# PSUM banks from one table of users, two heads per 32 columns, merged gate, rank and FFN projections, and new instruction lists in a one-core decoder block

## What is computed

```python
# 1 attention, 16 heads of 16, linear, with decay per head and a carried state
q, k = rotate(silu(x @ Wq)), rotate(silu(x @ Wk)); v = x @ Wv
scores = einsum('bthd,bshd->bhts', qi, ki) * D          # D: causal decay
o = scores @ v + (qi * decay_q) @ S;  S = lam_C * S + (ki * decay_k).T @ vi
o = group_rmsnorm(o * sigmoid(x @ Wg1 @ Wg2)) * weight
x = layernorm(x + o @ Wo)
# 2 experts: the token's number chooses one of 4; weights are ctx[e]
y = (silu(x @ Wg[e].T) * (x @ Wu[e].T)) @ Wd[e].T
x = layernorm(x + y)
# 3 FFN: positions are the FOUR sequences (l = 4), the 256 tokens are its batch
u = silu(prev(x) * conv_w[:, 0] + x * conv_w[:, 1])
q = rotate(silu(u @ Wq)); k = rotate(u @ Wk)            # 16 heads of 8
v = u @ Wv; g = u @ Wg
# each position picks one of two routes; causal sum over pairs (l, m), m <= l
o = sum_m (q_l . k_m) * same_route(l, m) * weight_l * v_m
x = layernorm(x + (silu(g) * head_norm(o)) @ Wout)
```

## Time and profile before

| | us |
|---|---|
| median of 3 runs | 193.52 |
| lowest and highest | 191.72, 193.52 |
| the profiled execution | 193.44 |
| its span, first to last instruction | 191.0 |
| around the span (193.44 - 191.0) | 2.44 |
| PE busy | 167.1 (87%) |
| DVE busy | 116.7 (61%) |
| POOL busy | 95.0 (50%) |
| ACT busy | 83.8 (44%) |

### The profile page before, as it was taken

How to read it: one execution, slowest core, us unless ns; L and a number is a source line. 1 busy time by engine, 2 the same in 40 slices (tenths; PEclk the granted TensorE clock), 3 DMA queues, 4 the chain that set the end, 5 groups by cost and what they waited for, 6 DMA issues and landing times.

```text
span 191.0 us, 3630 instructions
## 1 busy us (share of the span) xinstructions
PE 167.1 (87%) x1182; PEld 119.0 (62%) x1182; DVE 116.7 (61%) x318; ACT 83.8 (44%) x217; POOL 95.0 (50%) x175
## 2 busy tenths in 40 slices
PE   7699999999899999968968993989776999899870
PEld 7367476567577868747857892665352575588650
DVE  3156648995799779675312114260968959999731
ACT  2128362435155553344433522665546365542452
POOL 8957942431330566756640032624388524634682
PEclk9999799999999999999999999699999799999997
DMA  5999466000000001150537833211120000000113
GB/s 150 337 392 386 166 191 193 7 0 2 3 2 3 0 31 55 33 165 0 189 117 217 289 109 102 75 37 55 36 74 29 0 0 3 0 0 2 53 54 113
DMA packets 12417, 17.52 MB, mean 92 GB/s; under 512 B 1840, under 2 KB 8560, under 8 KB 12272
## 3 DMA queue, kind: packets, MB, share of 16 engines
q1 hardware_dynamic: 9056, 12.75, 20.5%
q10 hardware_dynamic: 2576, 2.46, 3.8%
q0 software_dynamic: 768, 2.10, 3.6%
HBM read 11.54 MB, written 5.77 MB: 91 GB/s over the span
## 4 chain that ended last, share of the span: by engine, by line
PE 54%; DVE 13%; POOL 10%; DMA 10%; issue 8%; ACT 4%; POOLq 0%; SPq 0%; DVEq 0%; ACTq 0%
PE bank L1462 20%; PE bank L1547 8%; PE bank L1457 4%; PE bank L1575 3%; PE bank L1692 3%; DMA xT<-in_x_turned 3%; DMA ys_d<-qkr 2%; PE bank L1767 2%; PE bank L1785 2%; PE bank L1569 2%; DMA yg<-ys_d,pos 2%; POOL yg L478 2%; POOL rstd L425 2%; PE bank L1677 2%; PE bank L1595 2%
## 5 line engine op out<-in xcount | busy, mean ns | idle before, releaser
L1462 PE MATMUL bank<-f_w,oT 128*128 128x512 f32 (+4 forms) x80 | 30.5, 534 | 2.4 <-ACT oT L773 2.4
L408 POOL TENSOR_TENSOR rsin<-qk,rope_tab 128x256 f32<-128x256 f32 x16 | 13.8, 879 | 23.5 <-ACT qk L643 23.5
L1462 PEld LDWEIGHTS bank<-f_w,oT 128*128 128x128 f32 x80 | 15.6, 207 | 14.6 <-issue 8.3
L1063 DVE TENSOR_TENSOR probs<-bank,con 128x512 f32<-128x512 f32 x32 | 20.6, 683 | 6.4 <-PE bank L1547 6.3
L1547 PE MATMUL bank<-qx,kT 32*128 32x256 f32 x128 | 18.4, 404 | 0.7 <-DVE probs L1063 0.7
L1462 PE MATMUL bank<-w_qk,xT 128*128 128x512 f32 x32 | 16.9, 655 | 1.6 <-DMA xT<-in_x_turned 1.6
L478 POOL DMA_INDIRECT yg<-ys_d,pos x8 | 8.1, 1007 | 18.7 <-DMA ys_d<-qkr 17.3
L1547 PEld LDWEIGHTS bank<-qx,kT 32*128 32x128 f32 x128 | 11.4, 188 | 6.7 <-issue 5.9
L1677 PE MATMUL bank<-xsT,slot_w 128*128 128x128 f32 x112 | 14.6, 284 | 0.2 <-issue 0.2
L1166 DVE TENSOR_TENSOR rsin<-rcos,bank 128x512 f32<-128x512 f32 (+1 forms) x8 | 4.9, 616 | 15.5 <-ACT rcos L744 15.5
L1677 PEld LDWEIGHTS bank<-xsT,slot_w 128*128 128x128 f32 x112 | 13.8, 197 | 0.7 <-issue 0.4
(11 more groups left out here) (155 smaller groups left out, 361.3 us busy)
## 6 DMA issues: line engine op xcount, KB each, us to landing
slot_w<-in_ctx_turned SPq DMA_DIRECT2D x14, 256.0 KB, 3.0
xs_d<-xs SPq DMA_DIRECT2D x2, 896.0 KB, 12.5
xs<-xs_d SPq DMA_DIRECT2D x6, 256.0 KB, 3.0
ys_d<-qkr ACTq DMA_DIRECT2D x6, 256.0 KB, 3.1
xT<-in_x_turned SPq DMA_DIRECT2D x4, 256.0 KB, 6.6
x_sb<-in_x SPq DMA_DIRECT2D x1, 1024.0 KB, 9.1
out<-x_sb SPq DMA_DIRECT2D x8, 128.0 KB, 1.7
w_qk<-in_w_qk ACTq DMA_DIRECT2D x1, 512.0 KB, 3.9
```

Source lines behind the costliest of these rows:

```text
L408: eng.tensor_tensor(dst[:, :, s, :], src[:, :, 1 - s, :], tab[:, :, s, :], ALU.mult)\
L1063: eng.tensor_tensor(probs[:, i % 2, :, :].rearrange("p (f r h) n -> p f r h n", f=KT, h=2)[:, :, g, :, :], bank[3 + g % 2][:, :].rearrange ...
L1462: last = eng.matmul(dst, lhsT[:, k, :], w[:, k, :], start=(k == 0), stop=(k == KT - 1))
```

## The change

- A table `BANKS` lists, for each of the eight banks, all its users in order; `at(kind, i)` gives the bank and `free(eng, kind, i)` waits for the reading of the user before it in the table. All fixed banks and their waits are gone, and buffers that were laid over others (`zsil`, `aT`, `ys`, `prev`, `conv`, `uT`) have their own memory.
- `scores(i)` is one step for all four 32-row groups into four banks. `attend(i)` is one step: two heads share 32 output rows (the values of each padded with zeros on the other's side and summed in PSUM). `oT` has 256 columns instead of 512, `turn_back` two transposes instead of four, `state` 128 columns instead of 256 per half, and its clearing is gone. `turn_q` and `turn_k` are one `turn_qk` in one bank.
- `gate_low` and `proj_gate` are once for all eight tiles, with four column or row groups. The gate is Tanh of half its input, and `gate_o` multiplies by (tanh + 1); the factor 2 goes into the root's epsilon.
- `rank_tokens` is two matmuls; DVE makes the running sums (`earlier_in`) first, in four more small steps. `inverse_root` has nine steps instead of eleven.
- The FFN projects each key once and rotates the query (`turn_query`, POOL, three instructions, for l < 3). `project_values` and `project_route` replace `project_step`: 384 or 512 and 400 or 272 columns.
- `keep_input` puts the residual's matmul first in each output group, as one matmul of up to 512 columns.
- All five lists are written anew; SP issues `fetch_second(0)` and `fetch_second(1)` ahead of the loads of chunk 1.

```diff
+BANKS = [
+    "qk.1 gate.2 qk.4 back.1 qk.6 on.0 sc.21 qkT.6 sc.26 sc.29 back.6 z.0 wo.6 y.1 xsT.5 z.5 xsT.7 f1.1 h2T.5 sum.0 fT.0",
...
+        def free(eng, kind, i):
+            if before_it[kind, i] is not None:
+                for name, value in last_read(*before_it[kind, i]):
+                    eng.wait_ge(S_(name), value)
...
-                eng.memset(state[:, :, :, :], 0.0).then_inc(S_("state_zeros"), 1)
...
+            def turn_query(j):
+                c, l = j // L, j % L
+                n = c * (L - 1) + l
+                eng.wait_ge(S_("fq_copied"), j + 1)
+                if n:
+                    eng.wait_ge(S_("q_turned"), 2 * n)
+                eng.tensor_tensor(q_parts[:, :, :].rearrange("p s (h d) -> p s h d", d=HK), ..., ALU.mult)
+                eng.wait_ge(S_("q_parts"), n + 1)
+                for half in range(2):
+                    eng.tensor_tensor(heads(fqr[:, c, l, :], HK)[:, :, a], ..., ALU.subtract)
...
+            def tanh_gate(n):
+                eng.wait_ge(S_("gate_made"), n + 1)
+                eng.activation(gate[:, 2 * n:2 * n + 2, :], two(at("gate", n)[:, :]), ACT.Tanh, scale=0.5)
...
+            def gate_low():
+                for k in range(KT):
+                    for n in range(4):
+                        last = eng.matmul(at("low", 0)[32 * n:32 * n + 32, 0:D], w_g1[:, k, :], xT[:, 2 * n:2 * n + 2, k, :],
...
+            def scores(i):
+                for g in range(4):
+                    free(eng, "sc", 4 * i + g)
                 for f in range(KT):
-                    for half in range(2):
-                        rows_ = slice(64 * r + 32 * half, 64 * r + 32 * half + 32)
+                    for g in range(4):
+                        rows_ = slice(32 * g, 32 * g + 32)
+                        last = eng.matmul(at("sc", 4 * i + g)[:, f * D:(f + 1) * D], kT[rows_, i % 2, f, :],
...
+            def attend(i):
+                free(eng, "o", i)
+                eng.wait_ge(S_("probs"), 4 * i + 4)
                 for f in range(KT):
+                    if i >= L:
+                        for n in range(4):
+                            eng.matmul(out_[n], state[:, i - L, f, 32 * n:32 * n + 32], qp[:, i % 2, f, :],
+                    for s in range(2):
+                        for n in range(4):
+                            last = eng.matmul(out_[n], v_sb[:, i % 3, 4 * f + n, s:s + 2, :].rearrange("p a e -> p (a e)"),
+                                              probs[:, i % 2, 8 * f + 2 * n + s, :], ...)
...
+                eng.matmul(at("rank", 0)[:, 0:n + m], ones[:, :], earlier_in[:, :, :].rearrange("p b e -> p (b e)"),
+                           start=True, stop=False)
+                eng.matmul(at("rank", 0)[:, 0:n], causal, onehot..., start=False, stop=True)
...
+            def project_route(j):
+                a, n = (0 if l == 0 else P), D + H + P * (l < 2)
+                project(at("f2", j)[:, 0:n], uT[:, j % 2, :, :], f_w2[:, :, a:a + n])
+            def project_values(j):
+                a, n = (0 if l == 2 else P), 3 * P + P * (l >= 2)
+                project(at("f1", j)[:, 0:n], uT[:, j % 2, :, :], f_w1[:, :, a:a + n])
...
+            def keep_input(g):
+                eng.wait_ge(S_("h2_done"), L * c + l1)
+                free(eng, "fout", g)
+                eng.matmul(at("fout", g)[:, 0:(l1 - l0) * D], ident, h2[...], start=True, stop=False)
```

More of the change, by code:

```diff
@@ L1861, in _ @@
[L1861 to L1874 removed]
+            project_o(1)
+            scores(5)
+            attend(4)
+            transpose_on(2)
+            transpose_on(3)
+            turn_qk(6)
@@ L1875, in _ @@
+            project_o(2)
+            project_o(3)
+            attend(5)
+            scores(6)
+            turn_back(4)
+            turn_qk(7)
+            proj_v(6)
+            turn_back(5)
+            scores(7)
+            proj_v(7)
+            attend(6)
+            attend(7)
             turn_back(6)
-            attend(7, 0)
+            turn_back(7)
+            turn_slots(0)
             transpose_on(4)
-            attend(7, 1)
+            transpose_on(5)
             project_o(4)
-            turn_back(7)
```

1083 lines of the change are left out of this document (473 added, 610 removed), and 7 rows, old and new, of the table BANKS.

## The result

The changed kernel takes 174.55 us (median of 4 runs, 172.41 to 175.71), the kernel before, measured with it, 193.52. The ratio of the two is 0.8958, 95% interval 0.8832 to 0.9084. The profiled execution took 175.22 us, its span is 173.4. Executions of this kernel differ in where TensorE's granted clock falls (0.965 on average in this one), so what follows compares stages, and names the clock of each.

What follows compares the result with a forecast made beforehand. In attention TensorE was taken to set the pace, with VectorE close behind. Stages of 71.0, 20.6, 32.7, 42.0 and 4.8 gave a 171.1 us span, with 2.44 around it 173.5 us; range 166 to 183.

Steps and rivals of the forecast that it cites:

- Stage 1: From the start to the end of the last attend: 80.83 us before, predicted 71.0, a gain of 9.8.
- the first mask at about 15.3: In attention, VectorE's first mask was to start at about 15.3 us, against 25.37 before.
- Rival 1: In attention, scores stay at two row groups at a time, so TensorE keeps 8.5 us more: 183 us; chance 0.08.
- Stage 2: From the last attend's end to chunk 1's slots on TensorE: 22.1 us before, predicted 20.6, a gain of 1.5.
- Stage 3: From chunk 1's slots on TensorE to the FFN's first pair product: 31.4 us before, predicted 32.7, 1.3 longer.
- The narrower projections at nothing: In the FFN, 2.6 us less projection work per chunk was taken as hidden; if TensorE were the bound, worth 5.2.
- Stage 4: From the first pair product to the last statistics: 51.9 us before, predicted 42.0, a gain of 9.9.
- Stage 5: From the last statistics to the span's end (last root, finish, store): 4.8 us, predicted to stay.
- Rival 2: In attention, waits for a bank's previous reader hold TensorE at 0.80 busy: 181.5 us; chance 0.15.
- Rival 3: In the FFN, POOL becomes the bound; 2.5 us of waits stay and 3.5 are added: 179.5 us; chance 0.17.
- Rival 4: Both engines pack better, with Stage 1 at 67 us and Stage 4 at 39: 166.5 us; chance 0.15.
- Rival 5: Gaps in more places often drop TensorE to 1.2 GHz, slower than before: 198.5 us at 25 us; chance 0.03.

Runs made afterwards that it cites:

- e9: Changed kernel with every score product issued twice into the same place: 181.91 us, ratio 0.9319 to the kernel before.
- e4: Changed kernel with the second item's weights for chunk 1 fetched behind the loads of chunk 1's slots: 176.21 us, ratio 0.9192 to the kernel before.
- b3: Changed kernel with token numbers loaded second, 8 filler products ahead of transpose_h2(0), and fetch_second(1) behind chunk 1's slot loads: 168.57 us, ratio 0.8716 to the kernel before.
- e2: Changed kernel with mark_experts moved later in VectorE's list, between rope_cos(1) and rope_add(1): 172.95 us.
- b2: e2 plus 8 and 5 unread filler products on TensorE ahead of transpose_h2(0) and slots_down(7): 173.95 us, ratio 0.9035 to the kernel before.
- e7: Changed kernel with the FFN's route projection issued twice for positions 0 and 1 of each chunk: 178.66 us.
- e5: Changed kernel without keep_input, the residual added last in its group of sums as before the change: 178.78 us.
- e6: Changed kernel with the rotation of the FFN query (turn_query) and its waits left out: 172.82 us, ratio 0.8851 to the kernel before.
- e8: Changed kernel with the gates as Sigmoid instead of Tanh of half the argument, constants adapted: 174.39 us, ratio 0.9075 to the kernel before.
- e1: Changed kernel with the 16 score products of each tile in another order: 173.86 us, ratio 0.904 to the kernel before.
- e3: Changed kernel with chunk 1's last expert item moved ahead of the first FFN step: 176.38 us, ratio 0.9158 to the kernel before.
- e10: Changed kernel with the 4 KB of token numbers loaded second instead of fifth: 172.2 us, ratio 0.8763 to the kernel before.

## Why the prediction was right, and where its steps were off

**Stage 1: the mark right, one input wrong.** Scores took 1.15 us a tile where I had 1.06; the work fell from 18.4 to 9.1 us, so 9.3 went where I had 8.5. The Trainium skill, TensorE: Matmul & The Clock Gate, section Measured speedup vs the span model, gave 1.12: its rule of 3.07 instead of 4 is nearer than mine, and the trace agrees with it. That VectorE would take over at 0.85 was too low a share; it reached 0.95. What failed is "the first mask at about 15.3". I followed rotation, transpose and scores, and did not follow mark_experts, which the new list moves ahead of all VectorE work, up to the DMA it waits for. With the fall of the clock behind it, the first mask came 4.5 us late. The two errors cancelled, and that the mark was met to 0.8 us is luck: 48 us of VectorE work from 15.3 at a share of 0.95, and attend(7) behind it, would have ended near 67, and with the tokens early it did (66.35). Rival 1 is refuted by the 1.15 us and, for its price, by e9.

**Stage 2: the gain was not there.** I had the last scatter at +15.1 us after the last attend; it was issued at +16.0 (86.20). And I took 2.5 us for its landing, as before, where it took 3.78. With the second item's weights fetched behind the slots it took 2.40 (e4) and 2.39 (b3). That this fetch, which now starts beside the scatter, is what slows it is shown by those two against 3.71 to 3.92 us in the eleven others; the step that failed is that I carried over a DMA time without asking what runs beside it. The other 0.9 us lies on POOL. It began the last two scale_o at +4.4, near my +4.6, but the last scatter came 11.6 us behind that. My own pieces (1.2, 5.0 and three scatters of 1.3) give 10.1, and the +15.1 I wrote allows 10.5; 0.83 us of the 11.6 is a wait for VectorE's statistics. No run varied it.

**Stage 3: right but for the clock.** Gather(4) at +22.3 and the 10.5 us from there (four gathers 5.2, two ln_scale 2.5, two rotations 2.8). Where TensorE kept its clock, gather(4) came at +22.28 (e2), +22.75 (b2) and +22.47 (b3), and the stage took 33.0, 33.5 and 33.2 against 32.7. From gather(4) on it was 10.75. In the changed kernel's own profile gather(4) came at +24.6, behind a granted clock of 0.51 from 110 to 116 us; that is 2.3 of the 2.7 us missed. An earlier step was wrong without harm: gather(0) was to come at +8.6 and came at +10.3, at +9.6 to +10.0 in the three with a kept clock, so the 1.1 us gained on the kernel before's +9.7 weren't there. I had priced the clock only as the rival that loses everything, and left it out of the forecast's own terms. "The narrower projections at nothing" was right for stage 4 and wrong for stage 3: e7 gives TensorE 5.3 us of such work back, and between gather(4) and the first pair product 2.3 us came back, at least 0.8 of them by the projections.

**Stage 4: 2.2 us better.** VectorE's work shrank from 41.27 us of 51.88 to 35.65 of 39.82, which is 5.6 less (I had some 6 net). Its idle time shrank from 10.6 to 4.2, that is 6.4; my terms for waits and for the residual held 3.8. So the waits were mis-sized: 6.4 is more than both far bounds together (4.1 and 1.3). keep_input belongs to these, and what it is worth is not shown (e5). TensorE's "about 32" was 34.6. The rotations cost 1.6 us and not 0.5 (e6), well inside their bounds of 0 and 6.

**Stage 5** was 5.2 for 4.8. **The table loads** at nothing: e8 agrees. **Rival 2**, the bank table coupling the engines: between 20 and 70 us TensorE is busy 0.92, and beyond e1 no order of it was varied; no wait for a bank stands out in the trace, but a table with other numbers wasn't tried. **Rival 3** is refuted by e6. **Rival 4** came half: stage 4 reached 39.8 for its 39, and stage 1 got to 66.35 for its 67 only with the tokens early. **Rival 5** didn't come: the four runs of the changed kernel had a mean clock of 0.959 to 0.986, the 25 other runs of the kernel before that are on record 0.965 to 0.984. Stages 1 and 3 lost about 2 us each to a fall.

## What to carry to other kernels

When lists are rewritten, follow the first instruction of every engine to the DMA it waits for: a 4 KB load issued fifth held back the engine that was about to become the bound. Once the bound moves to the engine that was second, price the old bound's savings only to where the two meet (5.2 of 8.4 us here), and look for the gain at the new bound's start. Where idle gaps of TensorE precede dense work, the falls of its clock belong in the sum; with fillers into a bank that is overwritten anyway it kept its clock, and with the two other fixes this was 6 us.

## What the runs showed of the hardware

The 13 profiles of the changed kernel and its variants show what stood before the falls of the clock, and that this alone doesn't decide them.

- In the five where TensorE idled 2.67 to 2.71 us ahead of the first transpose (the changed kernel, e1, e3, e5, e9) the clock from 14 to 20 us was 0.72. In the eight without that wait it was 1.00. Four of these eight (e4, e6, e7, e8) had begun slowly, 5.37 to 5.69 us for the first eight passes instead of 3.67, and came out ahead: the late projections filled the wait. Their code up to there is that of the other five. That these passes ran at half clock is read from their durations: the trace's first record of a granted clock starts 9.9 to 10.7 us into the span there and at 4.3 to 6.0 us in the nine others, and the rows count the time before it as 1.00.
- Ahead of transpose_h2(0) TensorE idled in every profile without fillers. The clock from 108 to 116 us was 0.56 to 0.91 in the ten with 1.54 to 3.23 us, and 1.00 in e2, with 1.27. In both with fillers it was 1.00.
- In stage 4 the wait for h2 ahead of the last transposes was 0.86 to 1.36 us in five profiles (e1, e3, e5, e9, e10), and all but e3 fell within 3 us of it; in the other eight it was under 0.5 and none fell. But e2, b2 and b3 have the same wait of 0.88 us ahead of a transpose in stage 3 and didn't fall.
- Behind the wait for chunk 1's slots (1.65 to 2.04 us in eleven profiles) the clock fell to 0.50 in e3, e6 and e7 and in no other, though e9 waited as long as e7 (1.99 us). This cost 1.6 to 1.7 us ahead of gather(0) in e3 and e7.
- In the kernel before the clock fell at 21 us although TensorE had been busy in all of the 11 us before.

The Trainium skill, TensorE: Matmul & The Clock Gate, section HAM oscillation — how this bites in real kernels, says that waits between bursts bring the clock down again; the first two points agree. The others don't settle it: a wait of 0.9 or 2 us was followed by a fall in some profiles and not in others, and the last fall had no wait before it. What decides between them is open.

The 128 score products over four row groups took 9.1 and 9.4 us in the two orders that were tried, where 18.4 were needed with two row groups at a time.
